# Softmax transposes taken from TensorE to VectorE and DRAM, with more of the next image's convolution inside the attention

## Chip, cores and metric

The kernel runs on one core of one Trainium2 chip. The metric is the device time of one execution in microseconds. The kernel before took 1656.85 us (median of three runs, 1656.78 to 1657.14).

## The reference

```python
def reference(x, ...):                       # x: 16 images, 512 channels, 32x32 pixels, f32
    # convolution: 32 models of 16 channels, each sees 144 rows: the image and 8 shifted copies of it
    hdn = relu(einsum('bmchw,mdc->bmdhw', perception, w1) + b1)        # 64 hidden rows per model
    x = x + einsum('bmdhw,mcd->bmchw', hdn, w2) + b2
    # attention over the 1024 pixels of an image
    theta, phi, g = (w @ x + b for each)                               # 512 -> 128 rows
    attn = softmax(theta^T phi)                                        # 1024 x 1024
    y = attn g
    return bn(w_w @ y + w_b) + x
```

## The kernel before, in words

All engines follow orders written out by hand, one loop body per image; semaphores join them.

**Convolution.** An image is worked in eight slots: two halves of the pixels times four groups of channels. A slot `s` has four pairs `q`. `hidden_main` (L316) makes two 64-row matmuls per pair, `hidden_shared` (L329) adds the rest for all four pairs, ScalarE's `relu` (L510) evicts them to `hidden`, `dx` (L341) multiplies by w2 into the one bank BANK_DX, VectorE's `sum_x1` (L611) adds the input image and leaves `x1`, and `round_x1` (L516) and `split_x1` (L618) make the two float32r parts `x1_hi` and `x1_lo`. `dx` of slot `s` waits for `sum_x1` of slot `s - 1` (L344).

**Attention.** `project` (L352) makes theta, phi and g in two halves, each with three float32r products; `bias_projection` (L522) and `split_projection` (L625) make their parts. For each of eight blocks of 128 pixels, `scores` (L363) fills two PSUM banks, `find_max` (L632), `exp_rows` (L530), `invert_sum` (L637) and `normalize` on GpSimd (L743) make a softmax row block of 128x1024. `transpose` (L378) turns it with eight TensorE transposes into bank 4 and 5, `round_transposed` (L538) and `split_transposed` (L642) write the two parts `pt_hi` and `pt_lo`; the same is done once with g (tau = 0). `attend` (L394) takes two blocks (a quarter `j` of 256 pixels), `round_y` and `split_y` make y's parts, `output` (L406) multiplies by w_w, `add_out` (L658) adds to `x1`, and `store_quarter` (L251) stores 512 KB.

**Order.** `batch` of TensorE (L432) works image n's projections, scores, transposes, attention and outputs, and fills in `hidden_main` of slots 0 and 1 of image n + 1 near its end; slots 2 to 7 of image n + 1 come after the attention with nothing else between. The loop body then starts again with the projections.

**DMA.** All transfers are issued by SyncE on one queue, in the order of `batch` at L256. `load_freed(n, grp)` (L238) waits until slot `4 + grp` of image n - 1 has been summed and loads the windows (copies of the padded image, 575 KB each) of image n that are free from then on: one window for group 0, five for group 1 (2.88 MB), four for group 2 (2.30 MB) and nine for group 3 (5.18 MB). Before `sum_x1` writes `x1` for image n + 1, VectorE waits for the stores of image n: `stored[0]` (quarters 0 and 1) ahead of slot 0 (L698), `stored[1]` (quarters 2 and 3) ahead of slot 4 (L702).

Of the kernel before, what the change touches and what calls it, by code (L numbers as in the profile page):

```python
# [10 lines left out]
P = 128  # L11
# [17 lines left out]
ROWS_HELD = 4  # L29
# [62 lines left out]
def conv_attention(nc, x, w_mains, w_shareds, w2_pairs, proj_t, ww, per_channel, out):  # L92
    with ExitStack() as ctx:
# [8 lines left out]
        x1_hi = sb("x1_hi", [P, BLOCKS, PIXELS], F32R)  # L102
        x1_lo = sb("x1_lo", [P, BLOCKS, PIXELS], F32R)
# [9 lines left out]
        probs = sb("probs", [P, 2, PIXELS])  # L113
# [14 lines left out]
        def in_arena(at, blocks, cols):  # L128
# [7 lines left out]
        pt_hi, pt_lo = (x1_lo[:, 2 * e:2 * e + 2, :].rearrange("p k n -> p (k n)").rearrange(  # L136
            "p (b c) -> p b c", b=QBLOCKS) for e in range(2))
# [15 lines left out]
        def hidden_bank(s, q):  # L153
            return (GROUP_PAIRS * s + q) % HIDDEN_BANKS
# [46 lines left out]
        t_rounded = sem("t_rounded")  # L201
        t_split = sem("t_split")
# [10 lines left out]
        PROJECTIONS = [(0, TH, 2), (0, PH, 3), (1, PH, 6), (0, G, 4), (1, G, 5), (1, TH, 6)]  # L213
# [4 lines left out]
        T_PER = 2 * (QBLOCKS + 1)  # L218
# [5 lines left out]
        def _(sp):  # L224
# [30 lines left out]

            def batch(n, has_next, has_second):  # L256
# [41 lines left out]
        def _(pe):  # L298
# [6 lines left out]
            def await_bank(n, s, q):  # L305

                i = GROUP_PAIRS * s + q
                if i >= HIDDEN_BANKS:
                    pe.wait_ge(hidden_ready, n * SLOT_PAIRS + i - HIDDEN_BANKS + 1)
                elif not (isinstance(n, int) and n == 0):  # L310
                    if s == 0:
                        pe.wait_ge(exp_done, (n - 1) * QBLOCKS + QBLOCKS - 1 + q // 2)
                    elif q == 0:
                        pe.wait_ge(t_split, n * T_PER)

# [25 lines left out]
            def dx(n, s):  # L341
                pe.wait_ge(hidden_ready, n * SLOT_PAIRS + (s + 1) * GROUP_PAIRS)
                if s > 0:
                    pe.wait_ge(x1_ready, n * SLOTS + s)  # L344
                elif not (isinstance(n, int) and n == 0):
                    pe.wait_ge(out_added, n * 8)
# [5 lines left out]
            def project(n, half, w, blocks):  # L352
                step = proj_step(half, w)
                bank = ps[:, PROJECTIONS[step][2], :]
                cols = slice(half * HALF, (half + 1) * HALF)
                for k in blocks:
                    mm(bank, wp_hi[:, w, k, :], x1_hi[:, k, cols], start=(k == 0), stop=False)  # L357
                    mm(bank, wp_hi[:, w, k, :], x1_lo[:, k, cols], start=False, stop=False)  # L358
                    last = mm(bank, wp_lo[:, w, k, :], x1_hi[:, k, cols], start=False, stop=(k == BLOCKS - 1))  # L359
                if blocks[-1] == BLOCKS - 1:  # L360
                    last.then_inc(projected, 1)
# [16 lines left out]
            def transpose(n, tau):  # L378
                for u in range(2):
                    if tau == 0:  # L380
                        src = g_t
                        if u == 0:
                            pe.wait_ge(proj_biased, n * 6 + 5)
                    else:
                        if u == 0:
                            pe.wait_ge(normalized, n * QBLOCKS + tau)
                        pe.wait_ge(t_split, n * T_PER + 2 * (tau - 1) + u + 1)
                        src = softmax_rows[(tau - 1) % ROWS_HELD]
                    for v in range(4):
                        c = (4 * u + v) * P  # L390
                        last = nc.tensor.transpose(ps[:, BANK_T + u, v * P:(v + 1) * P], src[:, c:c + P], ident[:, :])  # L391
                    last.then_inc(transposed, 1)

            def attend(n, j):  # L394
                if j > 0:
                    pe.wait_ge(out_added, n * 8 + 2 * j - 1)
                bank = ps[:, y_bank(j), 0:QUARTER]
                for m in range(QBLOCKS):
                    if m % 4 == 0:
                        pe.wait_ge(t_split, n * T_PER + 2 * (2 * j + 2) + m // 4 + 1)  # L400
                    mm(bank, g_hi[:, m, :], pt_hi[:, m, :], start=(m == 0), stop=False)  # L401
                    mm(bank, g_hi[:, m, :], pt_lo[:, m, :], start=False, stop=False)  # L402
                    last = mm(bank, g_lo[:, m, :], pt_hi[:, m, :], start=False, stop=(m == QBLOCKS - 1))  # L403
# [19 lines left out]
            def end_slot(n, s):  # L423
# [3 lines left out]
            def image_slot(n, s):  # L427
                for q in range(GROUP_PAIRS):
                    hidden_main(n, s, q)
                end_slot(n, s)  # L430

# [376 lines left out]
```

## Time and profile before

| | |
|---|---|
| median of three runs | 1656.85 us |
| the profiled execution | 1657.71 us, its span 1655.7 us |
| granted TensorE clock, mean | 0.992 |
| TensorE (PE) busy | 1617.6 us, 98% of the span |
| ScalarE (ACT) | 774.1 us, 47% |
| VectorE (DVE) | 706.1 us, 43% |
| GpSimd (POOL) | 243.3 us, 15% |
| DMA, all on one queue | 210.65 MB, its packets took 42.0% of the 16 engines' span |

PE is TensorE's matmuls, SPq the queue of SyncE. Matmuls are pipelined, so the durations of neighbours overlap; what a group costs TensorE is read from start to start. The granted clock is a share of full speed, 1.00 for 2.4 GHz and 0.50 for 1.2 GHz.

### The profile page before, as it was taken

How to read it: one execution, taken by the hardware profiler on the slowest of the kernel's cores; microseconds unless marked ns; L12 is line 12 of the kernel's file. 1: busy time of each engine (PE TensorE's matmuls, PEld its weight loads, DVE VectorE, ACT ScalarE, POOL GpSimd, SP SyncE). 2: the span in 40 equal slices, each digit the busy share in tenths (PEclk: the TensorE clock that was granted, in tenths of full speed). 3: DMA queues.
4: the chain of work that ended last, by engine and by line, in shares of the span. 5: the costliest groups of instructions: out<-in, count | busy, mean ns of one | idle time of the engine just before them, and what ended most of it. 6: DMA issues, size and time to landing. Idle time of an engine off the chain costs nothing.

```text
span 1655.7 us, 26446 instructions
## 1 busy us (share of the span) xinstructions
PE 1617.6 (98%) x9476; PEld 952.3 (58%) x9476; DVE 706.1 (43%) x1200; ACT 774.1 (47%) x1349; POOL 243.3 (15%) x134
## 2 busy tenths in 40 slices
PE   5899999999999999999999999999999999999998
PEld 1276482845738466483754838457384664837557
DVE  0154262543626345262542625335263452625436
ACT  1444454544455454454544545444554544545444
POOL 0021030200203012030210302002030110302103
PEclk8999999999999999999999999999999999999999
DMA  9641723618144181632617235181441716327101
GB/s 283 152 157 52 219 81 98 193 38 250 57 125 159 51 250 51 163 126 83 206 51 229 72 107 182 38 263 51 131 158 40 249 51 186 102 88 200 51 0 51
DMA packets 82238, 210.83 MB, mean 127 GB/s; under 512 B 7728, under 2 KB 42544, under 8 KB 82224
## 3 DMA queue, kind: packets, MB, share of 16 engines
q1 hardware_dynamic: 82224, 210.65, 42.0%
q8 instruction: 9, 0.15, 0.0%
q14 instruction: 5, 0.04, 0.0%
HBM read 177.06 MB, written 33.55 MB: 127 GB/s over the span
## 4 chain that ended last, share of the span: by engine, by line
PE 89%; issue 3%; DVE 3%; ACT 2%; DMA 2%; SPq 1%; DVEq 0%; ACTq 0%
PE ps L326 27%; PE ps L337 8%; PE ps L348 7%; PE ps L391 6%; PE ps L357 5%; PE ps L359 5%; PE ps L358 5%; PE ps L401 4%; PE ps L402 4%; PE ps L403 4%; PE ps L374 3%; PE ps L375 3%; PE ps L373 3%; PE ps L414 2%; PE ps L415 2%
## 5 line engine op out<-in xcount | busy, mean ns | idle before, releaser
L326 PE MATMUL ps<-windows,w_main 128*64 128x512 f32 x2048 | 489.8, 607 | 16.3 <-DMA windows<-in_x 14.6
L513 ACT ACTIVATE hidden<-ps,columns 128x512 f32<-128x512 f32 x512 | 310.2, 689 | 407.4 <-PE ps L337 407.4
L326 PEld LDWEIGHTS ps<-windows,w_main 128*64 128x64 f32 x2048 | 133.7, 137 | 313.2 <-issue 253.4
L746 POOL TENSOR_TENSOR probs<-probs,row_inv 128x1024 f32<-128x1024 f32 x64 | 121.3, 1895 | 1274.6 <-DVE row_inv L640 1274.6
L622 DVE TENSOR_TENSOR x_lo<-x,x_hi 128x512 fp32r<-128x512 f32 x128 | 88.7, 693 | 372.8 <-ACT x_hi L520 372.8
L549 ACT CAST x_lo<-ps 128x512 fp32r<-128x512 f32 x256 | 139.3, 590 | 120.3 <-PE ps L391 115.4
L634 DVE TENSOR_REDUCE neg_max<-ps 128x1 f32<-128x1024 f32 x128 | 155.9, 1218 | 86.8 <-PE ps L375 85.7
L651 DVE TENSOR_TENSOR x_lo<-ps,x_lo 128x512 fp32r<-128x512 f32 x256 | 164.3, 683 | 33.8 <-ACT x_lo L549 33.8
L357 PE MATMUL ps<-x_hi,wp_hi 128*128 128x512 f32 x384 | 156.2, 407 | 7.1 <-DVE x_lo L622 5.4
L614 DVE SCALAR_TENSOR_TENSOR x<-ps,columns,windows 128x512 f32<-128x512 f32 x128 | 96.0, 750 | 147.8 <-PE ps L348 147.8
L401 PE MATMUL ps<-x_lo,arena 128*128 128x256 f32 x512 | 149.5, 292 | 2.3 <-DVE x_lo L651 1.2
L359 PE MATMUL ps<-x_hi,wp_lo 128*128 128x512 f32 x384 | 150.7, 392 | 0.0
L358 PE MATMUL ps<-x_lo,wp_hi 128*128 128x512 f32 x384 | 150.4, 392 | 0.0
L337 PE MATMUL ps<-windows,w_shared 32*128 32x512 f32 x1024 | 146.0, 640 | 2.6 <-DMA windows<-in_x 2.6
L402 PE MATMUL ps<-x_lo,arena 128*128 128x256 f32 x512 | 144.6, 282 | 0.0
L403 PE MATMUL ps<-x_lo,arena 128*128 128x256 f32 x512 | 144.6, 282 | 0.0
L746 POOL TENSOR_TENSOR hidden<-hidden,row_inv 128x1024 f32<-128x1024 f32 x64 | 121.3, 1895 | 123.4 <-DVE row_inv L640 123.4
L348 PE MATMUL ps<-hidden,w2s 128*32 128x512 f32 x1024 | 137.3, 608 | 0.0
L663 DVE SCALAR_TENSOR_TENSOR x<-ps,shift,x 128x256 f32<-128x256 f32 x256 | 109.4, 474 | 29.8 <-PE ps L420 29.8
L401 PEld LDWEIGHTS ps<-x_lo,arena 128*128 128x128 f32 x512 | 97.6, 191 | 33.7 <-DVE x_lo L651 31.9
L373 PE MATMUL ps<-arena 128*128 128x512 f32 x256 | 104.4, 408 | 0.0
L357 PEld LDWEIGHTS ps<-x_hi,wp_hi 128*128 128x128 f32 x384 | 72.5, 189 | 52.7 <-issue 26.9
(60 smaller groups left out, 1844.8 us busy)
## 6 DMA issues: line engine op xcount, KB each, us to landing
windows<-in_x SPq DMA_DIRECT2D x208, 562.0 KB, 13.0
out<-x SPq DMA_DIRECT2D x64, 512.0 KB, 2.9
windows<-in_x SPq DMA_DIRECT2D x32, 421.5 KB, 8.9
windows<-in_x SPq DMA_DIRECT2D x32, 409.9 KB, 11.1
windows<-in_x SPq DMA_DIRECT2D x32, 281.0 KB, 11.6
windows<-in_x SPq DMA_DIRECT2D x32, 140.5 KB, 9.6
windows<-in_x SPq DMA_DIRECT2D x16, 280.8 KB, 19.1
windows<-in_x SPq DMA_DIRECT2D x16, 272.5 KB, 4.2
```

The costliest lines, as they stand in the source:

```text
L326: mm(ps[rows, hidden_bank(s, q), :], w_main[:, p, which, :], shifted(windows[:, w, :], unit // UNITS, half), start=True, stop=False, skip_ ...
L337: mm(ps[:, hidden_bank(s, q), :], w_shared[rows, grp, :], shifted(windows[rows, plain_of(unit), :], unit // UNITS, half), start=False, sto ...
L348: last = mm(ps[32 * q:32 * q + 32, BANK_DX, :], w2s[:, s % GROUPS * GROUP_PAIRS + q, :], hidden[:, q, :], start=True, stop=True)
L357: mm(bank, wp_hi[:, w, k, :], x1_hi[:, k, cols], start=(k == 0), stop=False)
L358: mm(bank, wp_hi[:, w, k, :], x1_lo[:, k, cols], start=False, stop=False)
L359: last = mm(bank, wp_lo[:, w, k, :], x1_hi[:, k, cols], start=False, stop=(k == BLOCKS - 1))
L401: mm(bank, g_hi[:, m, :], pt_hi[:, m, :], start=(m == 0), stop=False)
L402: mm(bank, g_hi[:, m, :], pt_lo[:, m, :], start=False, stop=False)
L403: last = mm(bank, g_lo[:, m, :], pt_hi[:, m, :], start=False, stop=(m == QBLOCKS - 1))
L513: activation(hidden[:, q, :], ps[:, hidden_bank(s, q), :], ACT.Relu, bias=b1s[:, column:column + 1]).then_inc(hidden_ready, 1)
L651: nc.vector.tensor_tensor(lo, src, hi.bitcast(F32), ALU.subtract).then_inc(t_split, 1)
L746: nc.gpsimd.tensor_tensor(rows, rows, row_inv[:, e].to_broadcast([P, PIXELS]), ALU.mult).then_inc(normalized, 1)
```

## The change

Each row block of the softmax stays in `probs` (three of them now), VectorE transposes it in place in 32x32 squares (`transpose_row`), one DMA writes it to the DRAM tensor `rows_out`, and a second one reads it back so that the squares land in their places (pieces of 1 KB). `round_row` and `split_row` then work on 128x1024 in SBUF in one instruction each, where there were two from PSUM. g goes the same way (`transpose_g`). `pt_raw` and `pt_lo` lie in `x1_lo`, `pt_hi` in `x1_hi`. TensorE makes no transposes any more except the first ones of w_w. `hidden` takes five banks instead of six. Six slots of image n + 1 (0 to 5) are worked inside the attention of image n. ScalarE's order follows the same pattern. In SyncE's order the fourth store comes behind the loads of groups 0 and 1.

```diff
-ROWS_HELD = 4
+ROWS_HELD = 3
...
-x1_hi = sb("x1_hi", [P, BLOCKS, PIXELS], F32R)
-x1_lo = sb("x1_lo", [P, BLOCKS, PIXELS], F32R)
+x1_hi = sb("x1_hi", [P, 2, BLOCKS, HALF], F32R)
+x1_lo = sb("x1_lo", [P, 2, BLOCKS, HALF], F32R)
...
-probs = sb("probs", [P, 2, PIXELS])
+probs = sb("probs", [P, ROWS_HELD, PIXELS])
...
+rows_out = nc.dram_tensor("rows_out", (QBLOCKS + 1, P, PIXELS), F32).ap()
...
+def squares(row):
+    return row.rearrange("p (a k c) -> p a k c", a=4, c=BLOCK)
...
+def pt_raw(i):
+    return x1_lo[:, i // 2 % 2, :, :].rearrange("p k n -> p (k n)")[:, i % 2 * PIXELS:(i % 2 + 1) * PIXELS]
+def pt_hi(j):
+    return x1_hi[:, j % 2, :, :].rearrange("p k n -> p (k n)").rearrange("p (m c) -> p m c", m=QBLOCKS)
...
-softmax_rows = [probs[:, 0, :], probs[:, 1, :], hidden_halves[:, 0, :], hidden_halves[:, 1, :]]
-g_t = hidden_halves[:, 1, :]
+g_raw, g_t = hidden_halves[:, 0, :], hidden_halves[:, 1, :]
...
-HIDDEN_BANKS, BANK_T, BANK_Y, BANK_DX = 6, 4, 6, 7
+HIDDEN_BANKS, BANK_Y, BANK_DX = 5, 6, 5
+FIRST_SLOT_BANKS = [4, 5, 7, 6]
...
-    return (GROUP_PAIRS * s + q) % HIDDEN_BANKS
+    return (GROUP_PAIRS * s + q) % HIDDEN_BANKS if s > 0 else FIRST_SLOT_BANKS[q]
...
-PROJECTIONS = [(0, TH, 2), (0, PH, 3), (1, PH, 6), (0, G, 4), (1, G, 5), (1, TH, 6)]
+PROJECTIONS = [(0, TH, 2), (0, PH, 6), (1, PH, 7), (0, G, 4), (1, G, 6), (1, TH, 7)]
...
+    def row_back(i):
+        return rows_out[i].rearrange("(a r) (b n) -> (r b) a n", a=4, b=4)
...
+    def send_row(n, i):
+        sp.wait_ge(transposed, n * QBLOCKS + i + 1)
+        sp.dma_start(rows_out[i], probs[:, i % ROWS_HELD, :]).then_inc(row_sent[i], 16)
+    def fetch_row(n, i):
+        sp.wait_ge(row_sent[i], (n + 1) * 16)
+        sp.dma_start(pt_raw(i).bitcast(F32).rearrange("p (a n) -> p a n", a=4), row_back(i)
+                     ).then_inc(row_landed[i], 16)
...
-        for j in range(QUARTERS):
-            store_quarter(n, j)
+        send_row(n, 0)
+        send_g(n)
+        fetch_row(n, 0)
+        send_row(n, 1)
+        fetch_g(n)
+        fetch_row(n, 1)
+        for i in range(2, 5):
+            send_row(n, i)
+            fetch_row(n, i)
+        send_row(n, 5)
+        store_quarter(n, 0)
+        fetch_row(n, 5)
+        send_row(n, 6)
+        store_quarter(n, 1)
+        fetch_row(n, 6)
+        send_row(n, 7)
+        fetch_row(n, 7)
+        store_quarter(n, 2)
         if has_second:
-            for grp in range(GROUPS - 1):
-                load_freed(n + 2, grp)
+            load_freed(n + 2, 0)
+            load_freed(n + 2, 1)
+        store_quarter(n, 3)
+        if has_second:
+            load_freed(n + 2, 2)
...
+        if i == GROUP_PAIRS or i >= 2 * HIDDEN_BANKS - 1:
+            pe.wait_ge(hidden_ready, n * SLOT_PAIRS + max(i - HIDDEN_BANKS, 0) + 1)
+        elif isinstance(n, int) and n == 0:
...
+        elif s > 0:
+            pe.wait_ge(exp_done, (n - 1) * QBLOCKS + QBLOCKS - (1 if hidden_bank(s, q) < 2 else 0))
...
-        elif not (isinstance(n, int) and n == 0):
-            pe.wait_ge(out_added, n * 8)
...
+    def attend(n, j, has_next):
...
             pe.wait_ge(out_added, n * 8 + 2 * j - 1)
+        else:
+            pe.wait_ge(g_split, n + 1)
+            if has_next:
+                pe.wait_ge(hidden_ready, (n + 1) * SLOT_PAIRS + GROUP_PAIRS)
+        pe.wait_ge(pt_split, n * QBLOCKS + 2 * j + 2)
...
+            mm(bank, g_hi[:, m, :], pt_hi(j)[:, m, :], start=(m == 0), stop=False)
+            mm(bank, g_lo[:, m, :], pt_hi(j)[:, m, :], start=False, stop=False)
+            last = mm(bank.rearrange("p (a c) -> p a c", c=BLOCK), g_hi[:, m, :], pt_lo(j, m),
+                      start=False, stop=(m == QBLOCKS - 1))
...
+        project(n, 0, TH)
         dx(n, SLOTS - 1)
+        project(n, 0, PH)
+        project(n, 1, PH)
+        project(n, 0, G)
         scores(n, 0)
         scores(n, 1)
+        project(n, 1, G)
+        scores(n, 2)
+        project(n, 1, TH)
+        scores(n, 3)
+        scores(n, 4)
+        if has_next:
+            mains(n + 1, 0, every)
             hidden_shared(n + 1, 0)
+        scores(n, 5)
+        if has_next:
+            mains(n + 1, 1, range(0, 1))
+        scores(n, 6)
+        attend(n, 0, has_next)
+        if has_next:
+            dx(n + 1, 0)
+            mains(n + 1, 1, range(1, 3))
+        outputs(n, 0)
+        scores(n, 7)
+        attend(n, 1, has_next)
+        if has_next:
+            mains(n + 1, 1, range(3, 4))
+            hidden_shared(n + 1, 1)
+        outputs(n, 1)
+        if has_next:
+            mains(n + 1, 2, every)
+            hidden_shared(n + 1, 2)
+        attend(n, 2, has_next)
+        if has_next:
+            dx(n + 1, 1)
+            mains(n + 1, 3, every)
+        outputs(n, 2)
+        if has_next:
+            dx(n + 1, 2)
+            hidden_shared(n + 1, 3)
+            image_slot(n + 1, 4)
+            mains(n + 1, 5, every)
+            hidden_shared(n + 1, 5)
+        attend(n, 3, has_next)
+        if has_next:
+            dx(n + 1, 4)
+        outputs(n, 3)
+        if has_next:
+            image_slot(n + 1, 6)
+            image_slot(n + 1, 7)
...
+        if q == 0 and s > 0:
+            act.wait_ge(dx_summed, n * SLOTS + s)
+        elif q == 0 and not (isinstance(n, int) and n == 0):
+            act.wait_ge(g_split, n)
...
+            act.wait_ge(row_sent[i - ROWS_HELD], (n + 1) * 16)
...
+    def round_row(n, i):
+        act.wait_ge(row_landed[i], (n + 1) * 16)
+        nc.scalar.copy(pt_hi_squares(i), squares(pt_raw(i).bitcast(F32))).then_inc(pt_rounded, 1)
+    def round_g(n):
+        act.wait_ge(g_landed, (n + 1) * 16)
+        nc.scalar.copy(g_hi[:, :, :].rearrange("p k (a c) -> p a k c", a=4), squares(g_raw)).then_inc(g_rounded, 1)
...
+        exp_rows(n, 2)
+        exp_rows(n, 3)
+        round_row(n, 0)
+        round_g(n)
+        exp_rows(n, 4)
+        if has_next:
+            relus(n + 1, 0, range(0, 2))
+        round_row(n, 1)
+        if has_next:
+            relus(n + 1, 0, range(2, 4))
+        exp_rows(n, 5)
+        round_row(n, 2)
+        exp_rows(n, 6)
...
+        round_y(n, 3)
+        if has_next:
+            for s in range(5, SLOTS):
+                relus(n + 1, s, every)
+                round_x1(n + 1, s - 1)
...
+        if grp == 0 and not (isinstance(n, int) and n == 0):
+            dve.wait_ge(stored[half], n * 32)
...
+    def transpose_row(n, i):
+        dve.wait_ge(normalized, n * QBLOCKS + i + 1)
+        if i == 0:
+            dve.wait_ge(projected, n * 6 + proj_step(0, G) + 1)
+        elif i == 2:
+            dve.wait_ge(projected, n * 6 + proj_step(1, TH) + 1)
+        elif i % 2 == 0:
+            dve.wait_ge(y_summed, n * QUARTERS + i // 2 - 1)
+        row = probs[:, i % ROWS_HELD, :]
+        nc.vector.transpose(row, row).then_inc(transposed, 1)
+    def transpose_g(n):
+        dve.wait_ge(proj_biased, n * 6 + proj_step(1, G) + 1)
+        nc.vector.transpose(g_t, g_t).then_inc(g_transposed, 1)
+    def split_row(n, i):
+        dve.wait_ge(pt_rounded, n * QBLOCKS + i + 1)
+        raw = squares(pt_raw(i))
+        nc.vector.tensor_tensor(raw, raw.bitcast(F32), pt_hi_squares(i).bitcast(F32),
+                                ALU.subtract).then_inc(pt_split, 1)
+    def split_g(n):
+        dve.wait_ge(g_rounded, n + 1)
+        hi, lo = (t[:, :, :].rearrange("p k (a c) -> p a k c", a=4) for t in (g_hi, g_lo))
+        nc.vector.tensor_tensor(lo, squares(g_raw), hi.bitcast(F32), ALU.subtract).then_inc(g_split, 1)
...
+        sum_x1(n, SLOTS - 1)
         split_projection(n, 0, TH)
+        split_x1(n, SLOTS - 1)
         split_projection(n, 0, PH)
         split_projection(n, 1, PH)
         find_max(n, 0)
+        find_max(n, 1)
         invert_sum(n, 0)
         invert_sum(n, 1)
+        transpose_row(n, 0)
+        transpose_g(n)
+        find_max(n, 2)
+        transpose_row(n, 1)
         split_projection(n, 1, TH)
+        invert_sum(n, 2)
+        find_max(n, 3)
+        find_max(n, 4)
+        transpose_row(n, 2)
+        invert_sum(n, 3)
+        split_row(n, 0)
+        split_g(n)
+        invert_sum(n, 4)
+        transpose_row(n, 3)
+        find_max(n, 5)
+        split_row(n, 1)
+        find_max(n, 6)
+        invert_sum(n, 5)
+        transpose_row(n, 4)
+        split_row(n, 2)
+        split_y(n, 0)
+        invert_sum(n, 6)
+        transpose_row(n, 5)
...
+        split_row(n, 5)
+        transpose_row(n, 7)
+        if has_next:
+            sum_x1(n + 1, 0)
+        split_y(n, 2)
...
+        split_y(n, 3)
+        add_outs(n, 3)
+        if has_next:
             for s in range(GROUPS, SLOTS - 1):
                 sum_x1(n + 1, s)
                 split_x1(n + 1, s)
```

## Rows read from the trace of the kernel before

**Rows 1.** The page: span, and the busy time of each engine.
```profile
span 1655.7 us, 26446 instructions
PE 1617.6 (98%) x9476; PEld 952.3 (58%) x9476; DVE 706.1 (43%) x1200; ACT 774.1 (47%) x1349; POOL 243.3 (15%) x134
```

**Rows 2.** The chain in order of time (start us, us, what): slot 5 of an image.
```profile
774.35 3.58 PE ps L326 x16
777.94 1.00 PE ps L348 x8
778.93 1.07 PE ps L337 x8
780.01 3.58 PE ps L326 x16
```

**Rows 3.** TensorE's timeline (start us, us, instruction): six score matmuls, transposes, one `attend`.
```profile
706.56 0.39 PE L373 MATMUL ps<-arena 128*128 128x512 f32 x1
...
707.92 1.03 PE L391 MATMUL ps<-ident,hidden 128*128 128x128 f32 x8
708.71 0.48 PE L373 MATMUL ps<-arena 128*128 128x512 f32 x1
...
728.13 0.28 PE L401 MATMUL ps<-x_lo,arena 128*128 128x256 f32 x1
...
731.01 1.03 PE L391 MATMUL ps<-ident,probs 128*128 128x128 f32 x8
```

**Rows 4.** VectorE's timeline: `find_max` of row block 0, images 0, 7 and 15.
```profile
105.98 1.23 DVE L634 TENSOR_REDUCE neg_max<-ps 128x1 f32<-128x1024 f32 x1 [5.36 <-PE ps L375]
...
808.46 1.22 DVE L634 TENSOR_REDUCE neg_max<-ps 128x1 f32<-128x1024 f32 x1 [5.37 <-PE ps L375]
...
1610.85 1.23 DVE L634 TENSOR_REDUCE neg_max<-ps 128x1 f32<-128x1024 f32 x1 [5.37 <-PE ps L375]
```

**Rows 5.** Timelines of ScalarE and GpSimd, row block 0 of image 7.
```profile
809.85 1.13 ACT L535 ACTIVATE probs<-ps,neg_max 128x1024 f32<-128x1024 f32 x1
...
811.35 1.90 POOL L746 TENSOR_TENSOR probs<-probs,row_inv 128x1024 f32<-128x1024 f32 x1 [71.81 <-DVE row_inv L640]
```

**Rows 6.** Groups by line: count, then busy us, mean ns; idle before.
```profile
L634 DVE TENSOR_REDUCE neg_max<-ps 128x1 f32<-128x1024 f32 x128 | 155.9, 1218 | 86.8 <-PE ps L375 85.7 <-issue 0.4
L622 DVE TENSOR_TENSOR x_lo<-x,x_hi 128x512 fp32r<-128x512 f32 x128 | 88.7, 693 | 372.8 <-ACT x_hi L520 372.8
L734 DVE TENSOR_TENSOR wp_lo<-probs,wp_hi 128x1536 fp32r<-128x1536 f32 x1 | 1.8, 1751 | 0.0
L549 ACT CAST x_lo<-ps 128x512 fp32r<-128x512 f32 x256 | 139.3, 590 | 120.3 <-PE ps L391 115.4
L600 ACT CAST wp_hi<-probs 128x1536 fp32r<-128x1536 f32 x1 | 1.5, 1497 | 0.0
L513 ACT ACTIVATE hidden<-ps,columns 128x512 f32<-128x512 f32 x512 | 310.2, 689 | 407.4 <-PE ps L337 407.4
```

**Rows 7.** SyncE's queue: group 1's issues, then KB and us to landing.
```profile
780.30 1.43 SPq L227 DMA_DIRECT2D windows<-in_x  x3
...
783.11 0.32 SPq L232 DMA_DIRECT2D windows<-in_x  x1
...
windows<-in_x SPq DMA_DIRECT2D x1, 409.9 KB, 8.7
...
windows<-in_x SPq DMA_DIRECT2D x1, 281.0 KB, 3.7
...
out<-x SPq DMA_DIRECT2D x64, 512.0 KB, 2.9
columns<-in_per_channel SPq DMA_DIRECT2D x1, 21.5 KB, 11.6
```

**Rows 8.** Stretches behind the prologue: length, busy by engine, PEclk, DMA share, GB/s.
```profile
79.00:84.00 5.00, 0.55 (x8) 0.00 (x0) 1.77 (x7) 4.30 (x6) 0.00 (x0) 1.00 1.01 245
...
86.00:91.00 5.00, 4.08 (x10) 3.21 (x11) 0.58 (x1) 0.00 (x0) 0.00 (x0) 0.50 1.00 342
```

More of the change, by code:

```diff
@@ L200, in conv_attention @@
         transposed = sem("transposed")
-        t_rounded = sem("t_rounded")
-        t_split = sem("t_split")
+        row_sent = [sem(f"row_sent_{i}") for i in range(QBLOCKS)]
+        row_landed = [sem(f"row_landed_{i}") for i in range(QBLOCKS)]
+        pt_rounded = sem("pt_rounded")
+        pt_split = sem("pt_split")
+        g_transposed = sem("g_transposed")
+        g_sent = sem("g_sent")
+        g_landed = sem("g_landed")
+        g_rounded = sem("g_rounded")
+        g_split = sem("g_split")
         y_summed = sem("y_summed")
@@ L421, in output, with mains, outputs, image_slot @@
                 last.then_inc(z_summed, 1)
-            def end_slot(n, s):
+            def mains(n, s, pairs):
+                for q in pairs:
+                    hidden_main(n, s, q)
+            def outputs(n, j):
+                output(n, j, 0)
+                output(n, j, 1)
+            def image_slot(n, s):
+                mains(n, s, range(GROUP_PAIRS))
                 dx(n, s - 1)
                 hidden_shared(n, s)
[L427 to L430, printed above, removed]
@@ L555, in round_y, with relus @@
                 nc.scalar.copy(y_hi[:, :], ps[:, y_bank(j), 0:QUARTER]).then_inc(y_rounded, 1)
-            def image_slot(n, s):
-                for q in range(GROUP_PAIRS):
+            def relus(n, s, pairs):
+                for q in pairs:
                     relu(n, s, q)
-                round_x1(n, s - 1)
             def batch(n, has_next):
+                every = range(GROUP_PAIRS)
                 bias_projection(n, 0, TH)
+                round_x1(n, SLOTS - 1)
                 bias_projection(n, 0, PH)
-                round_x1(n, SLOTS - 1)
@@ new lines, in batch @@
+                exp_rows(n, 5)
+                round_row(n, 2)
+                exp_rows(n, 6)
+                round_y(n, 0)
+                round_row(n, 3)
+                exp_rows(n, 7)
+                round_y(n, 1)
+                round_row(n, 4)
+                if has_next:
+                    relus(n + 1, 1, every)
+                round_row(n, 5)
+                round_y(n, 2)
+                if has_next:
+                    round_x1(n + 1, 0)
+                    relus(n + 1, 2, range(0, 3))
@@ new lines, in batch @@
+                round_row(n, 6)
+                if has_next:
+                    relus(n + 1, 2, range(3, 4))
+                    round_x1(n + 1, 1)
+                    relus(n + 1, 3, range(0, 2))
+                round_row(n, 7)
+                if has_next:
+                    relus(n + 1, 3, range(2, 4))
+                    round_x1(n + 1, 2)
+                    relus(n + 1, 4, every)
+                    round_x1(n + 1, 3)
+                round_y(n, 3)
[3 more added lines that the diff above has]
+                        round_x1(n + 1, s - 1)
@@ L594, in _ @@
             nc.scalar.preload_act_table(ACT.Exp)
-            for q in range(GROUP_PAIRS):
-                relu(0, 0, q)
+            relus(0, 0, range(GROUP_PAIRS))
             for s in range(1, SLOTS):
-                image_slot(0, s)
+                relus(0, s, range(GROUP_PAIRS))
+                round_x1(0, s - 1)
             act.wait_ge(w_l1_loaded, 16 * W_L1_DMAS)
@@ new lines, in batch @@
+                add_out(n, 0, 0)
+                split_row(n, 3)
+                find_max(n, 7)
+                add_out(n, 0, 1)
+                invert_sum(n, 7)
+                split_y(n, 1)
+                transpose_row(n, 6)
+                split_row(n, 4)
+                add_outs(n, 1)
+                split_row(n, 5)
+                transpose_row(n, 7)
+                if has_next:
+                    sum_x1(n + 1, 0)
+                split_y(n, 2)
+                if has_next:
+                    split_x1(n + 1, 0)
+                    sum_x1(n + 1, 1)
```

213 lines of the change are left out of this document (55 added, 158 removed).

## The prediction, made before the change was run

> **What bounds the kernel now.** I read the page's busy times first: TensorE is busy for 98% of the span, every other engine for less than half of it [rows 1]. The chain in order of time then shows TensorE's own instructions following one another without a gap through the slots [rows 2], so the time is the sum of what TensorE is given. From one `find_max` of row block 0 to the same one fifteen images later it is (1610.85 - 105.98) / 15 = 100.3 us per image; 106.0 lie before the first of them and 1655.7 - 1610.85 = 44.9 behind the last [rows 4]. This makes the frame of the sum: head + 15 periods + tail. The timelines give the pieces of a period: six score matmuls run from 706.56 to 707.92, 1.36 us, 0.227 each; eight transposes take 0.79 until the next matmul starts (707.92 to 708.71), and some 0.08 to fill up again; 24 matmuls of `attend` take 2.88 (728.13 to 731.01), 0.12 each [rows 3]. A slot is 3.58 + 1.00 + 1.07 = 5.65 [rows 2].
>
> **The transposes that go.** Nine per image (g and eight row blocks) at 0.87 are 7.8 us. About 1.3 us of a period are small waits and refills around them. What is left for TensorE is 100.3 - 7.8 - 1.3 = 91.2 us per image. If nothing else waited, that would be 137 us less, 8%. The rest of the change decides how much of it is kept.
>
> **Costs of the new operations.** The splits of a row: VectorE's subtraction takes 693 ns at 512 and 1751 at 1536 columns, so 1.22 at 1024; ScalarE's copy takes 590 and 1497, so 1.05 [rows 6]. VectorE's transpose is in no trace. Bounds: 0.7 us, the 512-column instruction, if it handled two elements at a time, and 2.4, twice the 1.22 of a 128x1024 reduction [rows 6]; I take 1.2, since all of VectorE's f32 instructions here lie on one line of about 1 ns per column. VectorE gains 9 x 1.2 + 9 x 1.22 and loses 18 half splits of 0.68, about 10 us more per image: it has room on average, but almost all its work lies in the first 42 us of attention, where my order has it busy nearly throughout. Each row makes a DMA out and one back. Out and in 1 KB pieces, 512 KB land 2.9 us after issue in an empty queue; a 281 KB load lands after 3.7 [rows 7], and with another 0.23 MB at 0.34 MB/us a row's load takes 4.3. A round trip is 7.3 us, if nothing is ahead of it.
>
> **Is something ahead of it?** The queue serves in order: 21.5 KB of `columns` took 11.6 us behind windows, and the last windows of group 1, whose first issue is at 780.30, land at 783.11 + 8.7 = 791.8 [rows 7]. That is 11.5 us for 2.88 MB, of which about 10.5 are movement, 0.27 to 0.29 MB/us. Two places follow.
>
> **Place 1, the fourth store.** In the new order SyncE issues group 1 as soon as slot 5 is summed (call this X, plus 0.3), and the fourth store some 6.5 us later, behind it in the queue. The store therefore lands at about X + 11.8, plus 1.3 for its own 512 KB: X + 13.1. `sum_x1` of slot 4 waits for it (`stored[1]`, 0.75 us long), and `dx` of slot 5 waits for that sum, at X + 13.9. TensorE has from X: `attend` 2.9, `dx` 1.0, two outputs of six matmuls 1.5, and the four pairs of slot 6, 3.6: it stands at `dx` at X + 9.1. Taking the landing half a microsecond earlier in the middle of its spread of about a microsecond, the wait is 4.6 us in each of fourteen images (the last but one loads no windows). Behind it are the rest of slot 6, slot 7 and the next image, since TensorE is in order; nothing else of TensorE's could run.
>
> **Place 2, the start of attention.** Count from the end of the scores of row block 0. `find_max`, exp and inverse take until 3.0 and the normalization 1.9 [rows 5, 6]: row 0 is ready at 5.0, transposed at 6.3, g at 7.4; only then comes `find_max` of row 2 (8.6), the transpose of row 1 (9.8) and theta's split (10.5). `scores` 4 needs that split and could start at 9.5: 1.0 us of waiting. The windows of group 3 still fill the queue until about 8.0 (10.4 MB of groups 1 to 3 at 0.29, as now). Row 0's send lands at 10.3, g's at 11.9; g's fetch is issued at 12.0 behind row 0's fetch and row 1's send and lands at 16.8. ScalarE rounds it (17.9) and makes exp 4 (19.1), VectorE splits it at 19.2; only then may `relu` of the next image write `hidden` (`g_split`). The first relu ends at 19.9 (0.69 [rows 6]); TensorE stands at slot 1's first pair since 17.8: 2.2 us. Then two more relus at 0.6 each in a row, row 1's rounding, two relus: `attend` 0 starts at 23.0 instead of 22.3. Later waits (row 3's split before `attend` 1, slot 4's last pair behind `round_row` 7) are 0.3 and 0.5. Together 4.7 us; exp 3 to 7, each held by the send of the row three before, come later than those sends and cost nothing; rows 6 and 7 have over 4 us to spare.
>
> **Head and tail.** The head loses half of g's projection in front of the scores, 12 x 0.227 = 2.7: 103.2. In the last image no convolution hides the round trips. Row 7 is transposed at about 39, returns at 46.5, is rounded and split at 49, `attend` ends at 52, and the 7 us from there to the end stay: 59.5 where 44.9 were.
>
> **Sum.** A period is 91.2 + 4.6 + 4.7 = 100.5, practically what it was. 103.2 + 15 x 100.5 - 4.6 (the period without windows) + 59.5 = 1665.6. To this comes the clock: behind the prologue, where TensorE had 0.55 us of work in 5 us, the granted clock was 0.50 (1.2 GHz) for the next 5 [rows 8], which costs half of that, 2.5 us. The new wait of 4.6 us is of that length. I take it that the clock falls in something under a third of the images, 0.7 us each, between 0 and 2.5: 10 us. The span is then about 1675. Profiled executions take 2.0 more than their span and the median of the runs stood 0.9 under the profiled one, so 1676; for a measurement I say **1675 us**.
>
> The Trainium skill speaks against the change in its own way: VectorE: DVE Perf Modes (Rules for kernel authors) sends 128x128 transposes to TensorE, because VectorE's stay within 32x32 blocks. Here the second DMA does the rest of the job, and its wait, not the squares, is what I charge.
>
> **Rival A, faster: the round trip and the store stay hidden.** If stores overtake windows, or the group lands sooner, place 1 is nothing: 14 x 4.6 and the clock's 10 go, 1675 - 74 = 1601. With half of place 2 gone too it is 1601 - 35 = 1566. For it: no row before shows a store behind windows, and VectorE's neighbouring instructions overlap by 0.08, of which some twenty are in place 2. Against it: `columns` [rows 7] was a different kind of tile but the same queue, and it waited. The point from which it decides: 1665.6 without the clock's share is 9.9 over the span of before, 0.7 in each of fourteen images, so with a wait of under 3.9 us in place 1 and no fall of the clock the kernel is the faster one. 34%.
>
> **Rival B, clearly slower: VectorE becomes the bound of the attention.** Three transposes stand in front of `scores` 4 and of g's send; at 2.4 each, 3.6 us come on top of place 2 (partly the same wait), and the later ones push `attend` 1 and 2. Take 3 us per image: 1675 + 45 = 1720. The same happens if VectorE and GpSimd hold each other up: eight normalizations of 1.9 [rows 5] now lie beside VectorE's subtractions of two SBUF tiles, and three collisions per image of a microsecond are 45 us too. No row has the two side by side. 20%. The Trainium skill, SBUF — State Buffer (Who interferes with whom), says that a VectorE instruction with two SBUF inputs and a GpSimd one that reads SBUF exclude each other for the whole instruction; by that rule this rival's second form happens wherever they meet.
>
> **Numbers.** The forecast itself has 46%, with a range of its own of 1645 to 1700: waits in the two places of a microsecond more or less each, and the clock between 0 and 2.5. About 0.2% (3.3 us) can be told from no change. Of the forecast's 46%, 36 are slower, 6 within, 4 faster; A is faster, B slower. Faster 38%, within 6%, slower 56%. The range reaches into A and B until a fifth is left out: 1586 to 1715.
>
> **What would show it.** Right: no transposes of rows on TensorE; at `dx` (second w2 product of the six late ones) a wait of 4 to 5 us for VectorE's `sum_x1`, that one waiting for the DMA `out<-x`, once per image, and the store's landing at 6 us or more instead of 2.9; low granted clock in some stretches behind it; TensorE's first pair of slot 1 waiting for ScalarE, that for the DMA that brings g; a tail of some 60 us; VectorE's transpose near 1.2. Wrong: stores landing in 3 us each time, or `sum_x1` waiting for `dx` alone. If the period is under 97 with these waits there, the 91.2 is what was wrong.

## The result, and the profile after

The changed kernel takes 1738.47 us (median of four runs, 1732.98 to 1742.15) where the kernel before took 1656.82 in the same comparison: a ratio of 1.050, 95% interval 1.046 to 1.054. The forecast was 1675 with a range up to 1715: the sign was right, the size was not. The profiled execution took 1739.32, its span 1737.5.

The page after (span; busy time of each engine), against [rows 1]; behind it the granted clock of the whole span, the DMA queue and four landing times (KB, median us from issue to landing), against [rows 7]:

```profile
span 1737.5 us, 23755 instructions
PE 1551.6 (89%) x8324; PEld 838.4 (48%) x8324; DVE 875.1 (50%) x1200; ACT 765.2 (44%) x1205; POOL 249.6 (14%) x134
...
q1 hardware_dynamic: 178992, 361.66, 64.2%
...
rows_out<-probs SPq DMA_DIRECT2D x128, 512.0 KB, 5.1
x_lo<-rows_out SPq DMA_DIRECT2D x128, 512.0 KB, 4.4
out<-x SPq DMA_DIRECT2D x64, 512.0 KB, 3.6
```

TensorE is busy for 66 us less, part of that at the low clock, and idles for 148 us more. Where it idles stands in its list of waits (total us, times, longest):

```profile
PE ps L417 <- DVE x L706: 77.5, 15, 6.9
PE ps L463 <- DVE x_lo L752: 24.2, 34, 5.8
PE ps L397 <- ACT hidden L585: 19.0, 16, 1.3
PE ps L397 <- ACT probs L608: 16.4, 15, 1.2
PE ps L448 <- DVE arena L720: 10.0, 15, 0.7
```

The first is place 1: `dx` (L417) waits for `sum_x1` (L706). VectorE's waits say what that one stands for: `DVE x L706 <- DMA out<-x`, 104.6 us in 15 times. The other four are place 2 and the tail. The timelines of slot 5 of image 7, which is worked in the period of image 6 (SyncE's queue, VectorE and TensorE, in order of time), show the mechanism as forecast:

```profile
797.70 1.41 SPq L254 DMA_DIRECT2D windows<-in_x  x3
...
800.98 0.45 SPq L262 DMA_DIRECT2D windows<-in_x  x1
...
804.24 0.42 SPq L280 DMA_DIRECT2D out<-x  x1
812.16 0.75 DVE L706 SCALAR_TENSOR_TENSOR x<-ps,columns,windows 128x512 f32<-128x512 f32 x1 [8.09 <-DMA out<-x]
...
812.97 1.93 PE L417 MATMUL ps<-hidden,w2s 128*32 128x512 f32 x8 [6.29 <-DVE x L706]
```

The store is issued at 804.24, 3.3 us behind the last of group 1, and `sum_x1` starts on its landing 7.9 us later, where [rows 7] have 2.9. This image is one of the slower ones: over the fourteen images with windows the landing takes 6.0 to 8.4 us, 7.0 on average, and `dx` waits 4.5 to 6.9, 5.45 on average; in the last period, without windows, the store lands in 2.9 and `dx` still waits 1.2. `dx` costs 1.93 instead of 1.00 [rows 2]: its clock is low. The stretches of the same period (length, then busy time of PE, PEld, DVE, ACT and POOL, PEclk, DMA share, GB/s):

```profile
793.00:806.70 13.70, 13.68 (x84) 6.74 (x80) 2.93 (x7) 5.48 (x10) 0.00 (x0) 1.00 0.76 217
806.70:813.00 6.30, 0.03 (x4) 0.03 (x5) 0.75 (x1) 0.05 (x1) 0.00 (x0) 0.76 0.60 156
813.00:817.00 4.00, 4.00 (x18) 0.86 (x20) 1.44 (x2) 0.64 (x2) 0.00 (x0) 0.53 0.00 0
817.00:836.30 19.30, 19.30 (x95) 11.80 (x94) 5.75 (x9) 9.16 (x15) 0.00 (x0) 1.00 0.96 315
```

TensorE is busy without a gap up to 806.7, idle for 6.3 us, and works the next 4 at 1.2 GHz. The markers of [rows 4] are now at 101.43 (image 0), 730.70, 836.29 (images 6 and 7, counted from 0) and 1670.81 (image 15): head 101.4, mean period (1670.81 - 101.43) / 15 = 104.6, tail 66.7. The period without windows, the last, is 98.5.

### The profile page after: what moved, and what is told of

Its sections match the earlier page's. It is cut to its first block, busy times and chain, and to the rows that moved or that the text cites. A ratio compares the mean times of both kernels' runs of the same rounds, so it can differ in the third digit from the quotient of the medians.

```text
span 1737.5 us, 23755 instructions
## 1 busy us (share of the span) xinstructions
PE 1551.6 (89%) x8324; PEld 838.4 (48%) x8324; DVE 875.1 (50%) x1200; ACT 765.2 (44%) x1205; POOL 249.6 (14%) x134
## 4 chain that ended last, share of the span: by engine, by line
issue 85%; POOL 12%; DMA 1%; DVE 1%; PE 1%; POOLq 0%; ACT 0%; DVEq 0%; SPq 0%
POOL probs L885 12%; DMA rows_out<-probs 1%; DMA x_lo<-rows_out 1%; DVE x_lo L752 0%; PE ps L463 0%; PE ps L465 0%; PE ps L464 0%; DVE probs L743 0%; ACT x_hi L613 0%; POOLq L883 0%; DVE x L770 0%; POOLq L896 0%; DVE arena L758 0%; DVE neg_max L725 0%; ACT y_hi L623 0%
## 5 line engine op out<-in xcount | busy, mean ns | idle before, releaser
L885 POOL TENSOR_TENSOR probs<-probs,row_inv 128x1024 f32<-128x1024 f32 x128 | 248.9, 1950 | 1459.2 <-DVE row_inv L731 1459.2
L417 PE MATMUL ps<-hidden,w2s 128*32 128x512 f32 x1024 | 148.9, 656 | 77.5 <-DVE x L706 77.5
L752 DVE TENSOR_TENSOR x_lo<-x_lo,x_hi 128x1024 fp32r<-128x1024 f32 x128 | 170.4, 1331 | 70.4 <-ACT x_hi L613 69.5
L706 DVE SCALAR_TENSOR_TENSOR x<-ps,columns,windows 128x512 f32<-128x512 f32 x128 | 95.3, 744 | 200.4 <-DMA out<-x 104.6
L608 ACT ACTIVATE probs<-ps,neg_max 128x1024 f32<-128x1024 f32 x128 | 142.8, 1116 | 102.7 <-DVE neg_max L725 98.3
L613 ACT CAST x_hi<-x_lo 128x1024 fp32r<-128x1024 f32 x128 | 134.1, 1047 | 113.5 <-DMA x_lo<-rows_out 113.5
L743 DVE STREAM_TRANSPOSE probs<-probs 128x1024 f32<-128x1024 f32 x128 | 157.8, 1233 | 46.1 <-PE ps L465 34.3
L463 PE MATMUL ps<-x_hi,arena 128*128 128x256 f32 x512 | 152.3, 298 | 24.4 <-DVE x_lo L752 24.2
L408 PE MATMUL ps<-windows,w_shared 32*128 32x512 f32 x1024 | 158.9, 692 | 2.6 <-DMA windows<-in_x 2.6
L465 PE MATMUL ps<-x_lo,arena 128*128 128x256 f32 x512 | 148.3, 290 | 0.0
L464 PE MATMUL ps<-x_hi,arena 128*128 128x256 f32 x512 | 146.8, 287 | 0.0
L593 ACT CAST x_hi<-x 128x512 fp32r<-128x512 f32 x128 | 80.5, 629 | 135.1 <-DVE x L706 135.1
L463 PEld LDWEIGHTS ps<-x_hi,arena 128*128 128x128 f32 x512 | 99.5, 194 | 60.4 <-issue 51.4
```

The costliest lines, as they stand in the source:

```text
L408: mm(ps[:, hidden_bank(s, q), :], w_shared[rows, grp, :], shifted(windows[rows, plain_of(unit), :], unit // UNITS, half), start=False, sto ...
L417: last = mm(ps[32 * q:32 * q + 32, BANK_DX, :], w2s[:, s % GROUPS * GROUP_PAIRS + q, :], hidden[:, q, :], start=True, stop=True)
L463: mm(bank, g_hi[:, m, :], pt_hi(j)[:, m, :], start=(m == 0), stop=False)
L743: nc.vector.transpose(row, row).then_inc(transposed, 1)
L752: nc.vector.tensor_tensor(raw, raw.bitcast(F32), pt_hi_squares(i).bitcast(F32), ALU.subtract).then_inc(pt_split, 1)
L885: nc.gpsimd.tensor_tensor(rows, rows, row_inv[:, e].to_broadcast([P, PIXELS]), ALU.mult).then_inc(normalized, 1)
```

## The experiments

Eleven kernels ran; the kernel before, measured beside them three times, took 1653.3, 1651.9 and 1656.6 us. Ratios are to it, with their 95% intervals. The heads (the time up to the first marker) of kernels with the same code for it lay between 95.8 and 102.6 us, so periods are compared beside totals, and differences of totals between these kernels are good to some microseconds.

### Is it the store's landing, and nothing else?

```diff
 store_quarter(n, 3):
-    sp.dma_start(out[n, ..., quarter 3], x1[...]).then_inc(stored[1], 16)
+    sp.dma_start(out[n, ..., quarter 3], w_main[...]).then_inc(stored_last, 16)
 sum_x1:
-    dve.wait_ge(stored[half], n * 32)
+    dve.wait_ge(stored[half], n * (16 if half else 32))
+    if half: dve.wait_ge(out_added, n * 8)
```

> Edit: the fourth store sends weights in place of the last quarter of the output (that quarter is not computed into the output), with a semaphore of its own, so that the same bytes move at the same moments but the sum of slot 4 waits for three stores only. My theory (the wait is the store's landing): 6.3 + 1.9 us an image go, 14 times, 1738 - 115 = 1622 us. Rival (an engine's own work bounds slots 4 and 5, or the late windows do): under 30 us go, at least 1708 us.

1625.5 us, ratio 0.984 (0.981 to 0.987). All wait of `dx` is gone, every period lies between 96.8 and 97.6 (mean 97.16), and the mean clock goes from 0.962 to 0.988. Place 1 and what hangs on it cost 113 us, and without it the change is a gain of 1.6%. The store itself is as slow as before (6.9 us on average); only nobody waits for it. VectorE and GpSimd do exactly the same work in this run: rival B as the cause of the loss is refuted.

### What delays the store: order, or a share of the engines?

The store ahead of group 1:

```diff
 load_freed(n + 2, 0)
-load_freed(n + 2, 1)
 store_quarter(n, 3)
+load_freed(n + 2, 1)
 load_freed(n + 2, 2)
```

> Edit: the fourth store is issued ahead of the next-but-one image's group 1 windows instead of behind them. My theory is that the 6.29 us of TensorE wait at slot 5 and the clock that falls with it (about 1.9 us an image) come from the store standing behind those windows in SyncE's queue. Then the store lands about 3 us after its issue instead of 7.9, the slot 4 sum is early, and 14 x 8.2 = 115 us go. But the group 1 windows are then issued some 4 to 7 us later and land in the first row sends of the next attention, which may cost up to 5 us an image. So: 1622 us if the shifted windows are harmless, about 1690 us if they give back 5 us an image. Rival 1 (the store is late because VectorE adds the outputs late, not because of the queue): about 1735 us. Rival 2 (VectorE or its port is the bound): about 1735 us, the wait only changes its place.

1677.9 us, ratio 1.013 (1.010 to 1.017). The store lands in 3.3 to 3.6 us and the `dx` waits fall from 77.5 to 27.4 us, but the first pair of slot 1 gives back a part, from 19.0 to 44.4:

```profile
PE ps L397 <- ACT hidden L585: 44.4, 15, 7.2
PE ps L417 <- DVE x L706: 27.4, 15, 2.1
```

Its periods run from 98.9 to 107.0. The windows' median landing time is 11.5 us here and 7.6 in the changed kernel: their backlog reaches into the sends of the first rows and of g. The send of g lands in 2.8 us in all fifteen periods of the changed kernel, and in up to 9.3 here; the longest wait of slot 1, 7.2 us, is in that same period. The time lies between the two that the expectation named, nearer to the second.

The store in a queue of its own:

```diff
 def store_last(n):
+    act.wait_ge(out_added, n * 8 + 8)
+    act.dma_start(out[n, ..., quarter 3], x1[...]).then_inc(stored[1], 16)   # behind relus(n + 1, 5)
```

> Edit: the fourth store is issued by ScalarE after the ReLUs of slot 5 of the next image, so it is in another queue than the windows; SyncE issues the windows of groups 0, 1 and 2 without standing at the store. If only the order in SyncE's queue delays the store, it lands about 4 us after its issue and the wait at slot 5 falls from 6.3 to about 3 us or less, with the clock held: 1738 - 14 x 5 = 1668 us, at least. If the two queues share the same 16 engines half and half while about 4 us of windows are left, the store still takes 6 to 7 us: 1715 to 1735 us. If the group 2 windows, issued earlier now, push it further: over 1740 us.

1736.5 us, ratio 1.050 (1.048 to 1.052): nothing gained. ScalarE's queue and VectorE in the period of image 6:

```profile
799.48 0.38 ACTq L626 DMA_DIRECT2D out<-x  x1
805.91 0.75 DVE L714 SCALAR_TENSOR_TENSOR x<-ps,columns,windows 128x512 f32<-128x512 f32 x1 [6.59 <-DMA out<-x]
```

From issue to `sum_x1` it is 6.4 us here; over the fourteen images the landing takes 6.0 to 7.9 us, 7.0 on average, just as in the changed kernel, and the `dx` waits are 78.0 in all (77.5 there): it isn't the place in one queue that counts, but what has been issued and not yet moved when the store comes, in whichever queue. That the engines share half and half was only estimated.

The store between the windows:

```diff
-load_freed(n + 2, 1)
+load_freed(n + 2, 1, slice(0, 3))
 store_quarter(n, 3)
+load_freed(n + 2, 1, slice(3, None))
```

> Edit: SyncE issues three of the five windows of group 1, then the fourth store, then the other two. The three are issued before VectorE has added the last outputs, so that the store has some 2 us of backlog ahead of it instead of about 5, and the windows behind it lose under 1 us where putting the store ahead of the whole group cost some periods 4 to 8 us at slot 1. My theory (bytes ahead of the store, first in first out): wait at slot 5 from 6.3 to 2 to 3 us, no fall of the clock, slot 1's wait stays at 1.1: 1738 - 14 x (3.8 + 1.9) = 1658 us. Rival (the landing of a store amid window traffic is slow for another reason than the queue's order): over 1700 us.

1651.5 us (ten runs), ratio 0.999 (0.998 to 1.000): moving two windows behind one store takes back the whole loss against the kernel before. Group 1's first part, the store, and VectorE's sum:

```profile
763.36 1.41 SPq L254 DMA_DIRECT2D windows<-in_x  x3
...
769.89 0.41 SPq L278 DMA_DIRECT2D out<-x  x1
...
773.50 0.75 DVE L705 SCALAR_TENSOR_TENSOR x<-ps,columns,windows 128x512 f32<-128x512 f32 x1 [3.78 <-DMA out<-x]
```

`sum_x1` starts 3.6 us after the store's issue, and slot 1's first pair waits 17.5 us in all, about as in the changed kernel (19.0). Expected was 1658. `dx` still waits 26.1 us in all, 1.8 on average in each of the fourteen images, as much as the distance to the 1625.5 of the run without the store's wait; 1.2 of the 1.8 stand in the last period too, where no window moves and the store lands in 2.9. Behind these waits, 1.7 to 2.0 us long, the low clock cost time in one image of the fourteen.

### The wait for the store, moved instead of shortened

```diff
+def dx_bank(s): return BANK_Y if s == 5 else BANK_DX
 dx:  s == 5 waits for out_added >= n * 8 - 1, s == 6 for x1_ready >= n * SLOTS + 5
```

> Edit: no transfer changes; the w2 product of slot 5 goes to the PSUM bank 6, free by then, so that TensorE needs the sum of slot 4 (which waits for the store) one slot later, 5.7 us, at the product of slot 6. My theory (the 6.3 us are a late store and nothing else): 6.3 - 5.7 = 0.6 us of wait stay, the clock holds: 1738 - 14 x (5.7 + 1.9) = 1632 us, below the kernel before. Rival (behind the store VectorE and ScalarE are late too, so slots 6 and 7 wait instead): 3 us or more of wait an image stay, 1670 us or more.

1697.7 us, ratio 1.029 (1.026 to 1.032): the expectation missed by 66 us, the rival came. `dx` no longer waits, the first product of slot 7 does:

```profile
796.48 0.75 DVE L712 SCALAR_TENSOR_TENSOR x<-ps,columns,windows 128x512 f32<-128x512 f32 x1 [7.10 <-DMA out<-x]
797.27 0.62 ACT L599 CAST x_hi<-x 128x512 fp32r<-128x512 f32 x1 [7.93 <-DVE x L712]
797.79 2.42 ACT L591 ACTIVATE hidden<-ps,columns 128x512 f32<-128x512 f32 x4
...
798.53 1.69 PE L400 MATMUL ps<-windows,w_main 128*64 128x512 f32 x4 [3.46 <-ACT hidden L591]
```

ScalarE stands at `round_x1` of slot 4 (7.93 us idle) with slot 6's ReLUs queued behind it; slot 7 waits 2.6 to 5.0 us in each of the fourteen images. So its order was changed too:

```diff
-relus 5, round_x1 4, relus 6, round_x1 5, relus 7, round_x1 6
+relus 5, relus 6, round_x1 4, round_x1 5, relus 7, round_x1 6
```

> Edit: as the run with the product of slot 5 in bank 6 alone, and ScalarE rounds the slot 4 sum after the ReLUs of slot 6 instead of before them. In the run without this ScalarE stood at that rounding for the store and slot 7's first matmul waited 3.5 us for ReLUs queued behind it. My reading (ScalarE's order hands the wait on): that wait goes, about 0.6 to 1 us stays at the product of slot 6: 1698 - 14 x 3 to 3.5, and the clock's share of 1 to 2 us an image = 1630 to 1655 us. Rival (slot 6's product or VectorE's sums are late by themselves): over 1680 us.

**1628.0 us, ratio 0.984 (0.981 to 0.987)**: no DMA is touched, the store is as late as ever, and `dx` waits 1.0 us in the whole run (0.6 at most). This version beats both kernels. Slot 5's bank with the store between the windows, and ScalarE's order left alone:

> Edit: both, the store between the windows of group 1 and the product of slot 5 in bank 6. My theory: no wait for the store is left, so the time is that of the run in which slot 4's sum did not wait for it: 1625 us, between 1620 and 1632. Rival (the windows issued later disturb slot 1 as they did with the store ahead of the group): 1640 us or more.

1630.1 us, ratio 0.986 (0.984 to 0.988). With the store early, ScalarE's order could stay as it was, and all periods are 97.0 to 98.1.

### What the low clock costs

```diff
 dx, s == 5:
+    pe.wait_ge(out_added, n * 8 - 1)
+    for _ in range(22):
+        mm(ps[:, BANK_Y, :], tp_hi[:, TH, 0:P], tp_hi[:, PH, 0:HALF], start=True, stop=True)
     pe.wait_ge(x1_ready, n * SLOTS + s)
```

> Edit: on the changed kernel, nothing else touched, TensorE makes 22 matmuls of 128x512 (5.0 us) that nobody reads in front of the w2 product of slot 5, where it would wait 6.3 us for the store. The wait as a whole stays. Theory: the granted clock no longer falls behind it, which is worth 1.9 us in each of 14 images: 1738 - 27 = 1711 us. Rival (the low clock costs nothing, since other engines set the pace of slots 5 and 6): 1738 us.

1708.9 us, ratio 1.033 (1.031 to 1.036). TensorE's timeline in the period of image 6, the products that nobody reads and then `dx`:

```profile
790.20 5.28 PE L417 MATMUL ps<-arena 128*128 128x512 f32 x22
795.41 1.06 PE L421 MATMUL ps<-hidden,w2s 128*32 128x512 f32 x8
```

The stretch around them and the one behind (columns as above):

```profile
790.60:797.00 6.40, 6.40 (x38) 4.16 (x36) 1.72 (x3) 0.62 (x1) 0.00 (x0) 1.00 0.44 128
797.00:816.90 19.90, 19.90 (x103) 11.92 (x96) 6.12 (x9) 9.24 (x15) 0.00 (x0) 1.00 0.94 302
```

`dx` takes 1.06 instead of 1.93, and the mean period is 102.69 instead of 104.63, 1.94 us less or 29 in all. That mean hides two things. In the last period, where there is only 1.2 us to wait, the 22 products cost 3.7 us of their own (102.2 instead of 98.5). In the fourteen others the delay in front of `dx` is the same (5.4 and 5.5 us on average) and from `dx` to the next marker it is 21.5 us instead of 23.8: the low clock costs 2.3 us per image, 32 in all.

### Place 2 and the tail: round trip, transposes, clock

```diff
-row_back(i): rows_out[i]...          # fetches wait for the send
+row_back(i): rows_in[i]...           # filled with weights once; no wait
```

> Edit: the rows and g are fetched from another DRAM tensor, filled once with weights at the start, and the fetch does not wait for the send (so attention multiplies weights instead of the softmax; all sends and fetches stay). It takes the round trip through DRAM out of the chain and leaves its traffic and every VectorE transpose. My theory: place 2 (the waits inside attention, about 3.9 us an image as measured) loses 1.5 to 2.5 us an image and the tail about 8 us, place 1 stays at 6.3 us: 1700 to 1710 us. Rival (the whole loss is the latency of the round trip, in the slots too): under 1660 us. Rival (the round trip is hidden): 1735 us, but for the tail 1730.

1699.2 us, ratio 1.027 (1.024 to 1.030). The period is 2.3 us shorter: the wait for exp 6 (`ACT probs`, 16.4 us in all) is gone, that for `x_lo` is 12.4 instead of 24.2. Slot 1's first pair still waits 15.1 of 19.0 us, so it is not mainly the wait of g's fetch for its send that holds it. The tail is 65.2: only 1.5 shorter where 8 were expected.

```diff
-row = probs[:, i % ROWS_HELD, :]
+row = probs[:, i % ROWS_HELD, 0:BLOCK]
```

> Edit: VectorE's nine transposes an image take 32 columns instead of 1024 (so the softmax rows and g are not transposed but for their first 32 columns); all transfers, splits and waits stay. It takes about 9 x 1.15 = 10 us an image from VectorE, nothing else. My theory: VectorE is not the bound; place 1 (6.3 us, the store) stays, and of the 4 us of place 2 the wait of scores 4 and part of the wait for exp 6 go, 1 to 2 us an image, and 3 to 5 us in the tail: 1738 - 14 x 1.5 - 4 = 1713 us. Rival B of the prediction (VectorE bounds the attention): at least 3 us an image go from the attention alone, under 1690 us.

1716.1 us, ratio 1.039 (1.035 to 1.042). VectorE is busy for 130 us less (745.3 instead of 875.1), and the kernel gains 22. The wait of `scores` 4 for theta's split is gone, and slot 1's pair waits 3.8 us instead of 19.0: it is mostly VectorE's transposes in front of g's send that this pair pays for. Tail 64.5, 2.2 us shorter where 3 to 5 were expected. Rival B's bound (under 1690 us) is missed by far. Of the 25 us between the two profiled executions 5.7 lie in the head, which this edit doesn't touch.

```diff
 last image only:
+keep_busy(12); scores(n, 5)  ...  keep_busy(20); attend(n, 2)  ...  keep_busy(12); attend(n, 3)
```

> Edit: on the kernel with both edits (1630 us), in the last image alone TensorE makes 44 matmuls of 128x512 that nobody reads, 12, 20 and 12 of them, in front of score block 5, attend 2 and attend 3, where it waits 3.9, 5.8 and 3.3 us. It asks how much of the tail's 66 us (59.5 forecast) is the low granted clock. Theory (the clock): the 12 us more that the same instructions take in the tail come down to a few, the tail loses 5 to 9 us: 1622 to 1626 us. Rival (the tail is the chain of row blocks 5 to 7 through VectorE, ScalarE and the transfers, whatever the clock): 1630 us or a little more.

1626.0 us (1624.8 to 1628.8), ratio 0.983 (0.980 to 0.985). The kernel it is to be held against, 1630.1 (1627.3 to 1630.4), was measured beside other runs of the kernel before, and the two ranges overlap, so the traces have to say it. The tail of the run with both edits, as one stretch:

```profile
1562.23:1628.10 65.87, 42.77 (x210) 36.37 (x208) 40.08 (x55) 21.52 (x31) 16.17 (x8) 0.84 0.50 176
```

And the same stretch of this run:

```profile
1562.83:1627.00 64.17, 47.56 (x254) 39.89 (x252) 41.45 (x55) 21.44 (x31) 15.12 (x8) 0.95 0.52 181
```

The clock goes from 0.84 to 0.95 and the tail loses 1.7 us, where 5 to 9 were expected. The three runs on the tail give 1.5 (no wait for the send), 2.2 (short transposes) and 1.7 us (clock). Kernels with the same code for the last image have tails of 65.4 to 66.7 us, so each of these is hardly more than that spread: each alone is worth little. How the 7 us beyond the forecast divide among them stays open: no run took away two.

## Why the prediction was wrong in size

The forecast span was 1675.6, the measured one 1737.5, 61.9 more:

- **TensorE's own work**, forecast 91.2 us per image: this is the largest term, and the step that failed. In the run without the store's wait the periods have 93.2 of work and 3.9 of waits, so +2.0 per period, some 30 us. The forecast took 1.3 us of "small waits and refills around" the transposes off the period. From start to start, the period before has 7.4 us of transposes, only 0.4 of waits and 92.5 of the rest, so these 1.3 us were not there to be saved. Another 0.7 came with the new order: the scores take 0.6, `attend` 0.3 and `hidden_main` 0.3 us more, the projections and the outputs 0.3 each less.
- **Clock**, forecast 0.7 us per image, "under a third of the images": +22. The row it came from, 5 us of work at 1.2 GHz behind a stretch of idling [rows 8], was the right one; but it happened in all fourteen images, at 2.3 us each. The choice of a third was the error: the prediction's own upper end, 2.5 us in each image, was near.
- **Place 1**, forecast 4.6 us in 14 images: right in place, mechanism and number of times; the waits are 77.5 us where 64.4 were forecast, +13. TensorE came to `dx` when it was said to (X + 9.3 in image 7, forecast X + 9.1), but the store takes 7.0 us to land where 6.3 were worked out. The forecast's own numbers, 13.9 less 9.1 less half a microsecond, give 4.3 and not 4.6. The cost of the wait, low clock included, is shown twice, by taking it away (113 us) and by moving it (110 us); 77.5 of waits and 32 of low clock make 109.
- **Place 2**, forecast 4.7: 4.0 per period, for instance in the period of image 6 (0.66 `scores` 4, 1.14 slot 1, 0.19 and 0.85 `attend`, 1.12 for exp 6), -10 in all. The sum was near; its make-up wasn't. Exp 6's wait for the send of row 3 was costed at nothing ("exp 3 to 7 ... cost nothing") and is 1.1 us.
- **Head** 101.4 for 103.2, **tail** 66.7 for 59.5: +5. Row 7 is normalized 38.8 us after the marker but transposed at 44.7, not 39, because VectorE's order puts it behind other work, row 5's split last, which waits for ScalarE and that for the fetch. That wait is the smaller part: with fetches that don't wait for the send, row 7 is still transposed at 43.8. Timelines of ScalarE and VectorE in the last image of the changed kernel:

```profile
1713.27 1.04 ACT L613 CAST x_hi<-x_lo 128x1024 fp32r<-128x1024 f32 x1 [4.12 <-DMA x_lo<-rows_out]
...
1714.34 1.23 DVE L752 TENSOR_TENSOR x_lo<-x_lo,x_hi 128x1024 fp32r<-128x1024 f32 x1 [1.86 <-ACT x_hi L613]
1715.49 1.24 DVE L743 STREAM_TRANSPOSE probs<-probs 128x1024 f32<-128x1024 f32 x1
```

- Sizes that held: the transpose 1.23 us (1.2), the send of g 2.8 (2.9), the fetch 4.4 (4.3), the row's split 1.22 when nothing is beside it.

The terms sum to 61, 1 short of the 62. They are read from one execution of each kernel.

**Rival A** (34%) had the right condition and the wrong time: with the store hidden, the runs give 1625 to 1630, above its 1601, mostly by the 2.0 us per image by which TensorE's own work was set too low. The point from which it was to decide fell by the same error: with waits of 1.8 us in place 1, well under the 3.9 allowed, the kernel only drew level (1651.5). And even a store that lands in 2.9 us leaves a wait of 1.2, not nothing. **Rival B** is not what happened. Its second form exists, once in each image and not three times: the split of row 0 and GpSimd's normalization of row 3 meet. In the tail:

```profile
1685.05 1.89 POOL L885 TENSOR_TENSOR probs<-probs,row_inv 128x1024 f32<-128x1024 f32 x1 [2.14 <-DVE row_inv L731]
1685.13 2.90 DVE L752 TENSOR_TENSOR x_lo<-x_lo,x_hi 128x1024 fp32r<-128x1024 f32 x1 [0.15 <-ACT x_hi L613]
```

The split takes 2.90 us instead of 1.2 and ends 1.1 behind the end of the normalization, as if it had begun only then. In the period of image 6 the split comes first:

```profile
744.99 1.23 DVE L752 TENSOR_TENSOR x_lo<-x_lo,x_hi 128x1024 fp32r<-128x1024 f32 x1
...
745.03 2.93 POOL L885 TENSOR_TENSOR probs<-probs,row_inv 128x1024 f32<-128x1024 f32 x1 [2.22 <-DVE row_inv L731]
```

Now the split takes its 1.23 and the normalization 2.93 instead of 1.89. So it is in all sixteen images: the one that starts second, nine times the split and seven times the normalization, takes as long as if it had waited for the first to end. That agrees with the rule of the Trainium skill, SBUF — State Buffer (Who interferes with whom), that two such instructions exclude each other. Nine splits of 2.9 us raise the mean of all 128 to 1.33, 14 us together, on an engine that is busy for half of the span. On the path it is worth next to nothing: in the run without the store's wait, the periods with a long split and those with a long normalization differ by 0.1 us on average.

## What to carry to other kernels

When a change puts a store behind loads, ask who waits for the store and how many bytes are issued and not yet moved when it is issued: here two of five windows moved behind one store were worth 87 us. A late result can also be taken off the critical path by giving the next product another bank, but then the order of every engine that handles the result has to move with it. Cost a wait of TensorE with the low clock behind it in every repetition (here 2.3 us behind each wait of 4.5 to 6.9; of fourteen waits of 1.7 to 2.0 us only one had any, 1.6 us), and sum the work left after a removal from start to start. A wait in one image is no measure for all: image 7's landing of 7.9 us stands beside a mean of 7.0.

## What was not expected of the hardware

- Another queue didn't shorten the store: it lands in 7.0 us on average with either queue, with the same waits in all (78.0 and 77.5 us).
- The same delay, some 5.4 us per image, cost 2.3 us more with TensorE idle than with it busy on products that nobody reads.
- A VectorE subtraction of two SBUF tiles and a GpSimd multiplication that met did not slow each other a little: the second one took 1.0 to 1.7 us more, each time.
- Up to the first marker the kernels, with nearly the same code there, took 95.8 to 102.6 us in the one profiled execution of each, a spread of 6.8 us. That need not be the kernels: the kernel before alone took 1649.8 to 1656.5 us in one series of thirteen runs. The fifteen periods of the 1628.0 us version lie within 1.1.
